# A transformer layer on one core: layer norms applied behind the projections, and one group's probabilities normalized by GpSimd

## The chip, the cores and the metric

The kernel runs on one core of one Trainium2 chip. The metric is the device time of one execution in microseconds. Where times are shown, they are the median of the runs beside their lowest and highest.

## The reference

x is 32 sequences of 512 rows of 256 float32 numbers. The layer is

```python
x = x + attn(layernorm(x), wq, wk, wv, wo, q_norm_w, k_norm_w)
x = x + ffn(layernorm(x), weight, gate_w, lora_U, lora_V)
```

with a layer norm without weights, (x - mean) / sqrt(var + 1e-5). attn has 16 query heads and 4 key and value heads of 64; q and k go through an RMS norm with a weight for each head (x * rsqrt(mean(x*x) + 1e-6) * w), a query sees itself and the 127 keys before it, and softmax runs over those. ffn is

```python
gate = softmax(xt @ gate_w.T)                       # 8 experts
base = xt @ weight.T                                # 256 x 256
t = einsum('nh,erh->ner', xt, lora_U)               # rank 16
out = base + (1/16) * einsum('ne,eor,ner->no', gate, lora_V, t)
```

## The kernel before

The 16384 rows are cut into 128 tiles of 128 rows; slot(T) = T % 4 is the place of tile T in its sequence. There is no loop that does one tile from end to end: each engine has a hand-written `step(T)`, a fixed list of operations on tiles T+4 to T-4, run for all T, and semaphores tie the engines together. Each engine does its list strictly in order, so an operation that waits holds everything behind it on that engine.

Products keep float32 precision by splitting both operands into a high and a low part of type fp32r and adding three matmuls (`three`, lines 627 to 629). The high part is written by ScalarE (`high_x`, `high_y`, `high_h`, `high_tg`, `high_weights`), the low one, the difference, by VectorE (`low_...`).

The path of a tile: the load into xs (SyncE's queue, line 170); mean and variance on VectorE (421 to 428); the power -0.5 on GpSimd (`x_rstd_power`, 215); xc = x - mean and xn = xc * rstd on GpSimd (220, 226); transposes of xn on TensorE (`transpose_x`, 637); projections to q (two halves of 512 columns) and k and v; ScalarE squares q and k, VectorE sums them (439, 461) and makes the mean squares (444, 467), GpSimd raises them to -0.5 (231, 237), VectorE scales (450, 473), TensorE transposes. v is copied out by ScalarE (298, 299).

Attention of a tile goes in four groups g of four heads: the scores (676), from slot 1 on a copy of the own half by ScalarE (`own_scores`, 323) and a merge by VectorE (481; in slot 0 one addition, 485), the maximum (491), the exponentials with their sums on ScalarE (330), the reciprocals (496), and the normalization of the probabilities: groups 0, 1 and 3 by one VectorE pass (`norm_probs`, 502), group 2 by four ScalarE activations (`normalise`, 339). TensorE transposes the probabilities (`transpose_probs`), ScalarE stores them as pT (345), GpSimd selects the part for the other keys (`select`, 253 and 255, not in slot 0), and TensorE multiplies with the values (695, 710).

Then come the projection with w_o, x1 = that + x (514), its statistics and h_rstd on GpSimd (519 to 526, 242), hn = (x1 - mean) * rstd by VectorE (`norm_h`, 531), its transposes (726), the ffn projection (ps_ffn: 256 columns of base, 128 of t, 8 of the gate), the gate's softmax (542, 361, 547, 552), tg (557), and `add_lora`, then ob = ps_ffn + x1 (569) and the store (195).

The order around the change. TensorE, in `step(T)`: the projections of T-2 with w_o, transposes of h(T-3), of k(T), ffn(T-3), transposes of x(T+1), attention and scores of group 0, transposes of the probabilities (T-1, 1), the first half of q(T+1), transposes of q(T), of tg(T-3), scores (T, 1), attention (T-1, 1), and then `transpose_probs(T - 1, 2)`; the second half of q(T+1) and the rest stand behind it. GpSimd, in the step of T-1 that runs beside it, has `select(T-1, 0)`, `x_rstd_power`, `low_value_difference`, `select(T-1, 1)`, `h_rstd_power(T - 2)`, `select(T-1, 2)`. VectorE reaches h_ve behind the merge of (T, 0), `gate_share`, `inverse(T-1, 3)`, `gate_t` and `low_y(T-1, 0)`, and does `norm_probs(T-1, 3)` right behind it. ScalarE has `gate_exp(T-3)` ahead of `own_scores(T, 0)`.

In the fill, `high_weights(0, 1, 2)` on ScalarE and `low_weights(0, 1, 2)` on VectorE stand ahead of all steps; VectorE's first statistics of x come behind them.

Of the kernel before, what the change touches and what calls it, by code (L numbers as in the profile page):

```python
# [26 lines left out]
CONSTANTS = 7  # L27
RING, DEEP, WIDE = 3, 4, 8
NORM_BY_ACT = (2,)
# [50 lines left out]
def layer(nc, x, w_qkv, w_o, w_ffn, w_v, norm_w, out):  # L80
    ctx = ExitStack()
    with ctx:
# [16 lines left out]
        ident, later_key, neg_later = sb("ident", [P, P]), sb("later_key", [P, P]), sb("neg_later", [P, P])  # L99
        minus_half = sb("minus_half", [P, HEADS])  # L100
# [3 lines left out]
        xc, xn = sb("xc", [P, DEEP, DIM]), sb("xn", [P, DEEP, DIM])  # L104
# [39 lines left out]
        s_s, s_own, s_merged, s_max, s_exp, s_rden, s_pn, s_pna = (sem(n) for n in ("scores_done", "own_scores_copied", "scores_merged", "max_done", "exp_done", "rden_done", "probs_normed", "probs_normed_by_act"))  # L144
        s_pt, s_pT, s_po, s_pv, s_yh, s_yl = (sem(n) for n in ("probs_transposed", "pT_stored", "pT_other_done", "pv_done", "yT_high", "yT_low"))
        s_o, s_x1, s_hst, s_hmv, s_hve, s_hrstd, s_hn, s_ht, s_hth, s_htl = (sem(n) for n in ("o_projected", "x1_done", "h_stats_done", "h_mean_done", "h_var_done", "h_rstd_done", "h_normed", "h_transposed", "hT_high", "hT_low"))
        s_ffn, s_gmax, s_gexp, s_grd, s_gate, s_tg, s_tt, s_tth, s_ttl, s_lv = (sem(n) for n in ("ffn_projected", "gate_max_done", "gate_exp_done", "gate_rden_done", "gate_done", "t_gated", "t_transposed", "tgT_high", "tgT_low", "lora_added"))
# [16 lines left out]

        @block.sync
        def _(sp):
            def load_x(T):
                if live(T):
                    wait(sp, s_x1, done(T - WIDE))
                    sp.dma_start(xs[:, T % WIDE], x[T * P:(T + 1) * P, :]).then_inc(s_x[T % WIDE], 16)  # L170

# [28 lines left out]
        def _(pool):  # L200
# [4 lines left out]
            pool.wait_ge(s_const, 4)  # L205
# [10 lines left out]

            def centre_x(T):
                if live(T):
                    pool.wait_ge(s_xmv, done(T))
                    pool.tensor_tensor(xc[:, T % DEEP], xs[:, T % WIDE], x_mv[:, T % DEEP, 0:1].to_broadcast([P, DIM]), ALU.subtract).then_inc(s_xc, 1)  # L220

            def norm_x(T):
                if live(T):
                    pool.wait_ge(s_xrstd, done(T))
                    pool.wait_ge(s_xc, done(T))
                    pool.tensor_tensor(xn[:, T % DEEP], xc[:, T % DEEP], x_rstd[:, T % DEEP].to_broadcast([P, DIM]), ALU.mult).then_inc(s_xn, 1)
# [49 lines left out]
        def _(act):  # L276
            def high_weights(*which):
                for n in which:
                    act.wait_ge(s_w[n], 128 if n == W_O else 16)
                    nc.scalar.activation(WEIGHTS[n][1], plain(n), ACT.Copy).then_inc(s_wh, 1)  # L280
# [588 lines left out]
```

## Time and profile before

| | us |
|---|---|
| median of 3 runs | 2423.46 (2421.21 to 2423.61) |
| the profiled execution | 2420.27 |
| its span, first to last instruction | 2418.6 |

| engine | busy us | share of the span |
|---|---|---|
| TensorE (PE) | 2380.1 | 98% |
| ScalarE (ACT) | 2160.9 | 89% |
| VectorE (DVE) | 2152.0 | 89% |
| GpSimd (POOL) | 1309.6 | 54% |

The profile is of one execution. PEld is TensorE's load of weights, beside PE. The end of a matmul is modelled, so a busy PE isn't PE at its peak; its starts are events. Lines such as L633 are lines of the kernel. "idle before <-" names what ended an engine's wait, by the semaphores.

### The profile page before, as it was taken

What the parts mean: (1) busy time and instruction counts of PE and PEld (TensorE: products, weight loads), DVE (VectorE), ACT (ScalarE), POOL (GpSimd) and SP (SyncE); (2) the same over time, 40 slices, a digit from 0 to 9 for tenths busy, and PEclk for the clock granted to TensorE, in tenths of its full rate; (3) what the DMA queues carried; (4) which work ended last, traced back from release to release, by engine and by line L of the source; (5) the groups of instructions that cost most, each with busy time, mean ns of one, the idle gap of its engine ahead of it and who ended that gap; (6) DMA issues with size and microseconds to landing.
All of it is one profiled execution on the core that took longest, in us unless ns stands there. A gap on an engine that the chain in (4) does not pass through costs nothing.

```text
span 2418.6 us, 70409 instructions
## 1 busy us (share of the span) xinstructions
PE 2380.1 (98%) x25856; PEld 1958.6 (81%) x25856; DVE 2152.0 (89%) x5736; ACT 2160.9 (89%) x7687; POOL 1309.6 (54%) x1771
## 2 busy tenths in 40 slices
PE   6999999999999999999999999999999999999997
PEld 4888888888888888888888888888888888888886
DVE  6899899999988999999999899989999998999886
ACT  5899989999998999899989989998999899899996
POOL 3555555555555555555555555555555555555542
PEclk9999999999999999999999999999999999999999
DMA  2000000000000000000000000000000000000000
GB/s 70 13 15 19 15 15 16 18 15 15 19 15 15 15 19 15 15 15 19 15 15 19 16 15 15 19 15 15 15 20 15 15 17 18 15 15 19 13 9 12
DMA packets 39729, 41.23 MB, mean 17 GB/s; under 512 B 4448, under 2 KB 38624, under 8 KB 39392
## 3 DMA queue, kind: packets, MB, share of 16 engines
q1 hardware_dynamic: 39392, 36.73, 5.0%
q8 instruction: 213, 3.49, 0.6%
q14 instruction: 124, 1.02, 0.1%
HBM read 19.93 MB, written 16.78 MB: 15 GB/s over the span
## 4 chain that ended last, share of the span: by engine, by line
PE 97%; issue 1%; ACT 1%; POOL 1%; DVE 1%; DMA 0%; SPq 0%; POOLq 0%
PE ps_a L633 17%; PE ps_scores L676 14%; PE ps_y L695 12%; PE ps_d L629 7%; PE ps_d L627 7%; PE ps_d L628 7%; PE ps_y L710 5%; PE ps_b L629 5%; PE ps_b L627 5%; PE ps_b L628 5%; PE ps_d L633 3%; PE ps_c L629 2%; PE ps_c L628 2%; PE ps_c L627 2%; PE ps_c L633 1%
## 5 line engine op out<-in xcount | busy, mean ns | idle before, releaser
L330 ACT ACTIVATE probs<-merged,neg_max 128x128 f32<-128x128 f32 x2048 | 796.0, 394 | 0.5 <-DVE neg_max L491 0.5
L253 POOL TENSOR_SCALAR_AFFINE_SELECT pT_other<-pT 128x256 f32<-128x256 f32 x384 | 173.1, 451 | 606.4 <-ACT pT L345 606.4
L237 POOL TENSOR_TENSOR q_r<-q_ve,minus_half 128x8 f32<-128x8 f32 x256 | 420.3, 1642 | 92.4 <-DVE q_ve L467 92.4
L676 PE MATMUL ps_scores<-kT,qT 64*64 64x192 f32 (+2 forms) x8192 | 415.2, 311 | 1.0 <-DVE merged L481 0.6
L330 ACT ACTIVATION_READ_ACCUMULATOR probs<-merged,neg_max 128x1 f32 x2048 | 396.5, 194 | 0.0
L481 DVE COPY_PREDICATED merged<-later_key,ps_scores 128x512 f32<-128x512 int32 x384 | 284.7, 741 | 106.2 <-ACT merged L323 106.2
L345 ACT ACTIVATE pT<-ps_a 128x512 f32<-128x512 f32 x512 | 306.2, 598 | 62.0 <-PE ps_a L633 61.1
L491 DVE TENSOR_REDUCE neg_max<-merged 128x4 f32<-128x512 f32 x512 | 346.5, 677 | 4.5
L695 PE MATMUL ps_y<-pT,values 128*64 128x128 f32 x4096 | 337.0, 285 | 1.8 <-ACT pT L345 1.8
L633 PE MATMUL ps_a<-ident,probs 128*128 128x128 f32 x2048 | 336.4, 287 | 0.0
L676 PEld LDWEIGHTS ps_scores<-kT,qT 64*64 64x64 f32 x8192 | 262.7, 133 | 60.6 <-issue 32.8
L627 PE MATMUL ps_d<-wo_h,yT_h 128*128 128x256 f32 x1024 | 309.0, 302 | 0.0
L633 PEld LDWEIGHTS ps_a<-ident,probs 128*128 128x128 f32 x2048 | 214.6, 140 | 101.8 <-issue 101.8
L695 PEld LDWEIGHTS ps_y<-pT,values 128*64 128x64 f32 x4096 | 213.2, 136 | 102.4 <-issue 100.1
L629 PE MATMUL ps_d<-wo_l,yT_h 128*128 128x256 f32 x1024 | 289.1, 282 | 0.0
L628 PE MATMUL ps_d<-wo_h,yT_l 128*128 128x256 f32 x1024 | 288.4, 282 | 0.0
L502 DVE TENSOR_TENSOR probs<-probs,rden 128x512 f32<-128x512 f32 x384 | 267.2, 696 | 8.7
L231 POOL TENSOR_TENSOR k_r<-k_ve,minus_half 128x4 f32<-128x4 f32 x128 | 129.6, 1012 | 217.0 <-DVE k_ve L444 217.0
L350 ACT ACTIVATE yT_h<-ps_y 128x256 fp32r<-128x256 f32 x512 | 197.1, 385 | 55.2 <-PE ps_y L710 39.5
L508 DVE TENSOR_TENSOR yT_l<-ps_y,yT_h 128x256 fp32r<-128x256 f32 x512 | 215.1, 420 | 31.6 <-ACT yT_h L350 26.3
L323 ACT ACTIVATE merged<-ps_scores 128x512 f32<-128x512 f32 x384 | 229.3, 597 | 8.9 <-PE ps_scores L676 2.4
L242 POOL TENSOR_TENSOR h_rstd<-h_ve,minus_half 128x1 f32<-128x1 f32 x128 | 119.8, 936 | 172.9 <-DVE h_ve L526 172.9
(114 smaller groups left out, 6175.7 us busy)
## 6 DMA issues: line engine op xcount, KB each, us to landing
xs<-x SPq DMA_DIRECT2D x128, 128.0 KB, 2.2
out<-ob SPq DMA_DIRECT2D x128, 128.0 KB, 1.7
w_plain<-w_qkv SPq DMA_DIRECT2D x3, 512.0 KB, 5.0
w_plain<-w_o SPq DMA_DIRECT2D x8, 128.0 KB, 5.3
w_plain<-w_ffn SPq DMA_DIRECT2D x1, 392.0 KB, 5.7
w_plain<-w_v SPq DMA_DIRECT2D x1, 128.0 KB, 4.9
nw<-norm_w SPq DMA_DIRECT2D x1, 1.0 KB, 5.5
```

Of the source, the lines that this page charges most:

```text
L237: pool.tensor_tensor(q_r[:, T % DEEP, c], q_ve[:, T % DEEP, c], minus_half[:, 0:8], ALU.pow).then_inc(s_qr[n], 1)
L330: last = nc.scalar.activation(probs[:, r, h], merged[:, r, h], ACT.Exp, bias=neg_max[:, r, h:h + 1], accum_out=den[:, r, h:h + 1])
L345: nc.scalar.activation(pT[:, ring(T, g)], ps_pT[:].rearrange("p (h q) -> p h q", h=REP), ACT.Copy).then_inc(s_pT, 1)
L481: nc.vector.copy_predicated(merged[:, ring(T, g)], later_key[:].bitcast(I32).unsqueeze(1).to_broadcast(every), ps_scores[:, :, 0:P]).then_ ...
L491: nc.vector.tensor_reduce(neg_max[:, ring(T, g)], merged[:, ring(T, g)], AX.X, ALU.max, negate=True).then_inc(s_max, 1)
L502: nc.vector.tensor_tensor(probs[:, r], probs[:, r], rden[:, r].unsqueeze(2).to_broadcast([P, REP, P]), ALU.mult).then_inc(s_pn, 1)
L627: nc.tensor.matmul(ps, stat_h, mov_h, start=first, stop=False, skip_group_check=onto_ended)
L628: nc.tensor.matmul(ps, stat_l, mov_h, start=False, stop=False, skip_group_check=onto_ended)
L629: return nc.tensor.matmul(ps, stat_h, mov_l, start=False, stop=last, skip_group_check=onto_ended)
L633: last = nc.tensor.transpose(ps[:, c * P:(c + 1) * P], src[:, c * P:(c + 1) * P], ident[:])
L676: last = nc.tensor.matmul(ps_scores[queries, 2 * half + c, first:end], qT[rows, T % 2, 2 * g + c, queries], kT[rows, g // 2, at + first:at ...
L695: last = nc.tensor.matmul(ps_y[HD * half:HD * half + HD, n, 0:P], values[:, T % WIDE, g // 2 * 2 + half], pT[:, ring(T, g), 2 * half:2 * h ...
```

## The change

- Four weights (the three parts of w_qkv and w_ffn) are centred once: TensorE multiplies a 128x128 matrix of 1/256 with each (two matmuls), which gives each column's mean on every partition, and VectorE subtracts it. Only then come the high and low parts. The banks used are cleared afterwards.
- x and x1 are transposed raw. `centre_x`, `norm_x` (GpSimd) and `norm_h` (VectorE) are gone.
- The factor rstd is applied later: in the copy of v (scale), in the exponential of the gate (scale), in the final sum (one scalar_tensor_tensor). For q and k it cancels in the RMS norm, whose epsilon becomes 1e-6 * (var + 1e-5), a new small VectorE operation, x_eps. The gate's maximum gets its factor in a new one, `gate_max_normed`.
- Group 2's probabilities are normalized by one GpSimd pass, `norm_by_pool`, between `h_rstd_power` and `select(T, 2)`, no more by ScalarE.
- The store of tile T-2 is issued behind the load of x(T+8), in place of the store of tile T.

```diff
@@ SyncE @@
-            for T in range(TILES):
+            for T in range(TILES + 2):
                 load_x(T + WIDE)
-                sp.wait_ge(s_ob, done(T))
-                sp.dma_start(out[T * P:(T + 1) * P, :], ob[:, T % 2]).then_inc(s_st[T % 2], 16)
+                store(T - 2)
@@ GpSimd @@
+            def norm_by_pool(T, g):
+                if live(T):
+                    r = ring(T, g)
+                    pool.wait_ge(s_rden, groups(T, g))
+                    pool.tensor_tensor(probs[:, r], probs[:, r], rden[:, r].unsqueeze(2).to_broadcast([P, REP, P]), ALU.mult).then_inc(s_pnp, 1)
...
             def step(T):
                 q_power(T + 1, 0)
                 select(T - 1, 3)
-                norm_x(T + 2)
                 k_power(T + 1)
                 q_power(T + 1, 1)
-                centre_x(T + 4)
                 select(T, 0)
                 x_rstd_power(T + 4)
                 low_value_difference(T + 1)
                 select(T, 1)
                 h_rstd_power(T - 1)
+                norm_by_pool(T, 2)
                 select(T, 2)
@@ ScalarE @@
+                    if n in CENTRED:
+                        act.wait_ge(s_wc, CENTRED.index(n) + 1)
...
+                    act.wait_ge(s_xrstd, done(T))
...
-                    nc.scalar.activation(g_exp[:, T % DEEP], ps_ffn[:, DIM + ER:FFN_OUT], ACT.Exp, bias=g_negmax[:, T % DEEP], accum_out=g_den[:, T % DEEP]).then_inc(s_gexp, 1)
+                    nc.scalar.activation(g_exp[:, T % DEEP], ps_ffn[:, DIM + ER:FFN_OUT], ACT.Exp, bias=g_negmax[:, T % DEEP], scale=h_rstd[:, T % DEEP], accum_out=g_den[:, T % DEEP]).then_inc(s_gexp, 1)
...
                 high_y(T - 1, 0)
-                normalise(T - 1, 2)
                 high_tg(T - 3)
@@ VectorE @@
-            nc.vector.memset(ps_scores[:], 0.0).then_inc(s_clear, 1)
+            def centre_weights(k):
+                dve.wait_ge(s_wm, k + 1)
+                w = plain(CENTRED[k])
+                nc.vector.tensor_tensor(w, w, mean_bank(k).unsqueeze(1).to_broadcast(w.shape), ALU.subtract).then_inc(s_wc, 1)
...
+                    nc.vector.tensor_scalar(x_eps[:, T % DEEP], x_mv[:, T % DEEP, 1:2], RMS_EPS, LN_EPS * RMS_EPS, ALU.mult, ALU.add).then_inc(s_xeps, 1)
...
+            def gate_max_normed(T):
+                if live(T):
+                    dve.wait_ge(s_gneg, done(T))
+                    dve.wait_ge(s_hrstd, done(T))
+                    nc.vector.tensor_tensor(g_negmax[:, T % DEEP], g_neg[:, T % DEEP], h_rstd[:, T % DEEP], ALU.mult).then_inc(s_gmax, 1)
...
                 maximum(T - 1, 1)
-                norm_h(T - 3)
                 add_x1(T - 4)
...
                 gate_max(T - 3)
+                gate_max_normed(T - 3)
                 low_x(T + 1)
...
-            low_weights(0, 1, 2)
+            for k in range(len(CENTRED)):
+                centre_weights(k)
+                if k < 3:
+                    low_weights(k)
+            dve.wait_ge(s_wc, len(CENTRED))
+            nc.vector.memset(ps_scores[:], 0.0).then_inc(s_clear, 1)
@@ TensorE @@
             def transpose_x(T):
-                pe.wait_ge(s_xn, done(T))
-                transpose_blocks(ps_xT, xn[:, T % DEEP], KC).then_inc(s_xt, 1)
+                pe.wait_ge(s_x[T % WIDE], 16 * (T // WIDE + 1))
+                transpose_blocks(ps_xT, xs[:, T % WIDE], KC).then_inc(s_xt, 1)
...
             def transpose_h(T):
-                pe.wait_ge(s_hn, done(T))
-                transpose_blocks(ps_hT, hn[:, T % 2], KC).then_inc(s_ht, 1)
+                pe.wait_ge(s_x1, done(T))
+                transpose_blocks(ps_hT, x1[:, T % DEEP], KC).then_inc(s_ht, 1)
...
+            def weight_means(k):
+                n = CENTRED[k]
+                pe.wait_ge(s_w[n], 16)
+                w = plain(n)
+                for c in range(KC):
+                    last = nc.tensor.matmul(mean_bank(k), mean_of[:], w[:, c], start=c == 0, stop=c == KC - 1)
+                last.then_inc(s_wm, 1)
```

## Rows read from the trace of the kernel before

**Rows 1.** Busy time by stretch: us and instructions (x) of each engine, clock, DMA.

```profile
25.00:50.00 25.00, 19.06 (x158) 13.17 (x160) 19.16 (x43) 16.92 (x58) 10.31 (x11) 0.80 0.01 1
...
200.00:1000.00 800.00, 800.00 (x8762) 660.25 (x8756) 723.53 (x1934) 726.97 (x2595) 443.82 (x599) 1.00 0.05 16
```

**Rows 2.** Timeline, one TensorE step, T-1 in slot 0: start, length, engine, operation.

```profile
1154.00 0.88 PE L676 MATMUL ps_scores<-kT,qT 64*64 64x192 f32 x16
...
1154.45 0.27 ACT L361 ACTIVATE g_exp<-ps_b,g_negmax 128x8 f32<-128x8 f32 x1 [0.55 <-DVE g_negmax L542]
...
1154.95 0.60 ACT L323 ACTIVATE merged<-ps_scores 128x512 f32<-128x512 f32 x1
...
1156.26 1.27 ACT L339 ACTIVATE probs<-probs,rden 128x128 f32<-128x128 f32 x4
...
1157.21 0.15 DVE L526 TENSOR_SCALAR h_ve<-h_mv 128x1 f32<-128x1 f32 x1
1157.28 0.68 DVE L502 TENSOR_TENSOR probs<-probs,rden 128x512 f32<-128x512 f32 x1
...
1157.44 0.94 POOL L242 TENSOR_TENSOR h_rstd<-h_ve,minus_half 128x1 f32<-128x1 f32 x1 [4.09 <-DVE h_ve L526]
...
1158.74 0.66 PE L633 MATMUL ps_a<-ident,probs 128*128 128x128 f32 x4
```

**Rows 3.** The same timeline in slot 2 (five rows), slot 3, slot 1.

```profile
1117.71 0.27 ACT L361 ACTIVATE g_exp<-ps_b,g_negmax 128x8 f32<-128x8 f32 x1 [0.79 <-DVE g_negmax L542]
...
1117.96 0.59 ACT L323 ACTIVATE merged<-ps_scores 128x512 f32<-128x512 f32 x1
...
1119.77 0.41 POOL L255 TENSOR_SCALAR_AFFINE_SELECT pT_other<-pT 128x256 f32<-128x256 f32 x1
...
1120.46 0.94 POOL L242 TENSOR_TENSOR h_rstd<-h_ve,minus_half 128x1 f32<-128x1 f32 x1 [0.27 <-DVE h_ve L526]
...
1122.18 0.66 PE L633 MATMUL ps_a<-ident,probs 128*128 128x128 f32 x4
...
1139.14 0.94 POOL L242 TENSOR_TENSOR h_rstd<-h_ve,minus_half 128x1 f32<-128x1 f32 x1 [0.24 <-DVE h_ve L526]
...
1140.68 0.66 PE L633 MATMUL ps_a<-ident,probs 128*128 128x128 f32 x4
...
1175.92 0.94 POOL L242 TENSOR_TENSOR h_rstd<-h_ve,minus_half 128x1 f32<-128x1 f32 x1 [0.67 <-DVE h_ve L526]
...
1177.23 0.66 PE L633 MATMUL ps_a<-ident,probs 128*128 128x128 f32 x4
```

**Rows 4.** Timeline of the fill.

```profile
2.07 0.29 POOL L209 TENSOR_SCALAR_AFFINE_SELECT neg_later<-neg_later 128x128 f32<-128x128 f32 x1
...
5.41 1.06 ACT L280 ACTIVATE wqkv_h<-w_plain 128x1024 fp32r<-128x1024 f32 x1 [3.33 <-DMA w_plain<-w_qkv]
...
6.58 3.78 DVE L416 TENSOR_TENSOR wqkv_l<-w_plain,wqkv_h 128x1024 fp32r<-128x1024 f32 x3 [4.57 <-ACT wqkv_h L280]
...
10.40 0.42 DVE L421 BATCH_NORM_STATS2 x_stats<-xs 128x6 f32<-128x256 f32 x1
...
11.69 0.55 POOL L215 TENSOR_TENSOR x_rstd<-x_ve,minus_half 128x1 f32<-128x1 f32 x1
...
13.30 0.61 POOL L226 TENSOR_TENSOR xn<-xc,x_rstd 128x256 f32<-128x256 f32 x1
...
14.06 0.66 PE L633 MATMUL ps_d<-ident,xn 128*128 128x128 f32 x2 [14.06 <-POOL xn L226]
...
15.57 0.43 DVE L421 BATCH_NORM_STATS2 x_stats<-xs 128x6 f32<-128x256 f32 x1 [2.88 <-DMA xs<-x]
...
16.32 0.42 DVE L433 TENSOR_TENSOR xT_l<-ps_d,xT_h 128x256 fp32r<-128x256 f32 x1
...
17.40 0.63 PE L628 MATMUL ps_d<-wqkv_h,xT_l 128*128 128x512 f32 x1
...
17.83 0.63 PE L629 MATMUL ps_d<-wqkv_l,xT_h 128*128 128x512 f32 x1
```

More of the change, by code:

```diff
@@ L26 @@
 MASKED = -1e30
[L27 removed]
+CONSTANTS = 8
 RING, DEEP, WIDE = 3, 4, 8
[L29 removed]
+NORM_BY_POOL = (2,)
 def live(t):
@@ L170, in load_x, with store @@
                     sp.dma_start(xs[:, T % WIDE], x[T * P:(T + 1) * P, :]).then_inc(s_x[T % WIDE], 16)
+            def store(T):
+                if live(T):
+                    sp.wait_ge(s_ob, done(T))
+                    sp.dma_start(out[T * P:(T + 1) * P, :], ob[:, T % 2]).then_inc(s_st[T % 2], 16)
             def load_weight(n):
@@ L332, in exps @@
                         last.then_inc(s_exp, 1)
-            def normalise(T, g):
-                if live(T):
-                    r = ring(T, g)
-                    act.wait_ge(s_rden, groups(T, g))
-                    for h in range(REP):
-                        last = nc.scalar.activation(probs[:, r, h], probs[:, r, h], ACT.Copy, scale=rden[:, r, h:h + 1])
-                    last.then_inc(s_pna, 1)
             def store_pT(T, g):
@@ L443, in k_mean_square @@
                     dve.wait_ge(s_kms, done(T))
-                    nc.vector.tensor_scalar(k_ve[:, T % DEEP], k_ms[:, T % DEEP], 1.0 / HD, RMS_EPS, ALU.mult, ALU.add).then_inc(s_kve, 1)
+                    dve.wait_ge(s_xeps, done(T))
+                    nc.vector.tensor_scalar(k_ve[:, T % DEEP], k_ms[:, T % DEEP], 1.0 / HD, x_eps[:, T % DEEP], ALU.mult, ALU.add).then_inc(s_kve, 1)
             def norm_k(T):
@@ L466, in q_mean_square @@
                     dve.wait_ge(s_qms[n], done(T))
-                    nc.vector.tensor_scalar(q_ve[:, T % DEEP, c], q_ms[:, T % DEEP, c], 1.0 / HD, RMS_EPS, ALU.mult, ALU.add).then_inc(s_qve[n], 1)
+                    dve.wait_ge(s_xeps, done(T))
+                    nc.vector.tensor_scalar(q_ve[:, T % DEEP, c], q_ms[:, T % DEEP, c], 1.0 / HD, x_eps[:, T % DEEP], ALU.mult, ALU.add).then_inc(s_qve[n], 1)
             def norm_q(T, n):
@@ L526, in h_mean_and_var @@
                     nc.vector.tensor_scalar_add(h_ve[:, T % DEEP], h_mv[:, T % DEEP, 1:2], LN_EPS).then_inc(s_hve, 1)
-            def norm_h(T):
-                if live(T):
-                    dve.wait_ge(s_hrstd, done(T))
-                    nc.vector.tensor_scalar(hn[:, T % 2], x1[:, T % DEEP], h_mv[:, T % DEEP, 0:1], h_rstd[:, T % DEEP], ALU.subtract, ALU.mult).then_inc(s_hn, 1)
             def low_h(T):
@@ L568, in add_x1 @@
                     wait(dve, s_st[T % 2], 16 * (T // 2))
-                    nc.vector.tensor_tensor(ob[:, T % 2], ps_ffn[:, 0:DIM], x1[:, T % DEEP], ALU.add).then_inc(s_ob, 1)
+                    nc.vector.scalar_tensor_tensor(ob[:, T % 2], ps_ffn[:, 0:DIM], h_rstd[:, T % DEEP], x1[:, T % DEEP], ALU.mult, ALU.add).then_inc(s_ob, 1)
             def step(T):
```

54 lines of the change are left out of this document (29 added, 25 removed).

## The prediction

> **What bounds the kernel now.** I read the windows first [rows 1]. Behind the fill, TensorE is busy 800.00 us of 800.00, at a full granted clock, while VectorE (723.53) and ScalarE (726.97) have 9% to spare and GpSimd (443.82) nearly half. So making VectorE or ScalarE lighter buys nothing there; only two things can move the time: a new wait that is long enough to reach TensorE's in-order queue, and the fill ahead of the loop, where TensorE is busy 19.06 of 25 us and the mean granted clock is 0.80.
>
> Next I read the timeline of one TensorE step, from the scores of group 0 of tile T to the transposes of group 2's probabilities of tile T-1 [rows 2] (here T-1 is the first tile of a sequence, slot 0), and of the three other slots [rows 3]. What to see: the scores end at 1154.88; ScalarE's copy starts at 1154.95, VectorE's merge and four short operations follow, and h_ve is done at 1157.36. GpSimd's h_rstd starts at 1157.44 and takes 0.94, to 1158.38. TensorE reaches the transposes of group 2 at 1158.74. This chain hangs on the scores of the same step, so it keeps its place relative to TensorE however long a step gets.
>
> **The change, part by part.**
>
> *Group 2's pass goes from ScalarE to GpSimd, behind h_rstd.* This is the term that decides. Before, ScalarE did it in 1.27 us from 1156.26 in that step, ended over a microsecond before the transposes, and waited only for the reciprocals. Now it stands in GpSimd's in-order queue behind h_rstd_power(T-1) of the same step, so it can't begin before 1158.38, 0.36 us ahead of the transposes that need it. TensorE will wait in every step; the price is
> stall = (start of h_rstd) + 0.94 + (the pass, d) - 0.04 + (release) - (start of the transposes).
> 0.04 is the overlap at which one GpSimd operation follows another. The release is 0.15: in the fill xn ended at 13.91 and its transposes started at 14.06 [rows 4].
>
> The trace has no 128x512 tensor_tensor on GpSimd. Nearest is xn, 128x256 with a broadcast operand, in 0.61 us [rows 4]. From below d is 0.61 (all of it fixed), from above 1.22 (all of it proportional). The selects grow from 0.29 (128 columns) [rows 4] to 0.41 (256 columns) [rows 3]: 0.12 to 0.13 for 128, so some 0.16 is fixed, and (0.61 - 0.16) x 2 + 0.16 = 1.06. I take d = 1.10, between that and the doubling, nearer the first. Could d be below the lower bound? Twice the elements don't take less.
> The Trainium skill (GPSIMD Engine Reference, section 3.1) gives 4497 ns for a tensor_tensor of 2048 fp32 columns on GpSimd and advises VectorE for such work; by that 512 columns are at least an estimated 1.12 us, and the sum would be 3 us longer.
>
> With d = 1.10 the sum in front of the transposes is 0.94 + 1.06 + 0.15 = 2.15 from h_rstd's start:
> slot 0: 1157.44 + 2.15 - 1158.74 = 0.85;
> slot 1: 1175.92 + 2.15 - 1177.23 = 0.84;
> slot 2: 1120.46 + 2.15 - 1122.18 = 0.43;
> slot 3: 1139.14 + 2.15 - 1140.68 = 0.61.
>
> *Small VectorE operations ahead of h_ve.* x_eps and gate_max_normed are 128x1 operations; h_ve is one of 0.15. An independent one adds some 0.07 (h_ve is followed by the next operation 0.07 behind its start, 1157.21 to 1157.28); a dependent one about 0.2 (0.15 and the wait for its own semaphore). Both stand ahead of gate_exp, which is queued on ScalarE ahead of the copy of the scores. In slot 0 the copy starts 0.50 behind gate_exp's start and needs only 0.25 (slot 2, where it follows at once: 1117.71 to 1117.96): cover 0.25, so 0.02 is left. In slot 2 all 0.27 shows. In slot 3 there is no such copy (0). In slot 1 I set the 0.27 against what the two GpSimd passes taken away release, and take -0.04. The stalls become 0.87, 0.80, 0.70 and 0.61, mean 0.75; in 127 steps 95 us.
>
> *What is removed.* centre_x and norm_x (0.61 each on GpSimd), norm_h (one VectorE pass a tile), ScalarE's four activations (1.27 a tile). All lie beside a TensorE that never waits [rows 1]: 0. Lighter queues don't shorten the chain, since its start is the scores' end. The transposes of x and x1 now wait for the load and for x1, both earlier than before: 0.
>
> *Scales moved into operations that are there* (store_v, gate_exp, the final add, the mean squares): same count and shape, 0; x_rstd and x_eps are four tiles ahead. *The SP queue*: out is stored two rounds later in program order, so a load of x stands only behind x1 of its tile. Stores come behind load_x(T+8), which waits for x1(T); ob(T-2) is ready in the same step, and its buffer is needed two steps later. Loads stay over one step ahead of their statistics. 0.
>
> *The fill.* Before: ScalarE rounds the first weight at 5.41, VectorE has three differences from 6.58 on (3.78 us), the first statistics start at 10.40, and the fourth round, held by the load of x, ends in low_x at 16.32; the first projection runs at once [rows 4]. After: each weight goes TensorE, VectorE, ScalarE, VectorE, in turn. Means: an fp32 matmul of 512 columns isn't in the trace. The fp32r one is issued every 0.43 us here, at the 1.2 GHz level (17.40 to 17.83). From below the fp32 one costs the same. From above: the fp32 scores are eight matmuls of 192 columns, four side by side on quarters of the array, in 0.88 [rows 2], so 384 columns in a row, 2.3 ns each at full clock, 4.6 at half: 2.35 for 512. That row holds one tail of some 0.27 besides, without which it is 1.6 and 1.65; I take 1.7. Two of them make 3.4, so centring can start at 8.9. Per weight then 1.25 (centre, like a difference, 1.23) + 1.15 (rounding 1.06) + 1.25 = 3.7, three times: 20.0; the centring of w_ffn 0.95; the clearing of the scores, moved here, 0.9; the norm weights 0.2: statistics start at 22.1. Four rounds of 0.85 (0.75 before, from the statistics at 15.57 to low_x at 16.32; x_eps and its wait on top): 25.5. low_x is 9.1 us later than 16.32. The matmul's bounds make this 6.6 to 10.4. The later parts of the fill hang on the same chain as before, shifted. TensorE has been idle since some 14 us by then, so the first projections run at 1.2 GHz as before.
>
> *The drain*: two gate chains with one more dependent operation, 0.2 each: 0.4.
>
> **The sum.** 2418.6 + 95 + 9.1 + 0.4 = 2523.1 us span; the profiled execution took 2420.27, 1.7 more than its span: 2524.8. The median of the runs shown is 2423.46, 3.2 above it and 0.13% away; I add 1.2 of that and say 2526.
>
> **The rivals.**
> A, the forecast: late pass, chance 0.70, with d from 0.87 to 1.22 between 2496 and 2540.
> B, the pass is short enough. Were d 0.61 and h_rstd 0.55, as x_rstd is at 11.69 [rows 4], the chain would be 0.55 + 0.57 + 0.15 = 1.27 from h_rstd's start; slots 0 and 1 leave 1.30, slot 3 more. Then only the fill is left: 2433. Against it: h_rstd takes 0.94 where VectorE's norm_probs overlaps it (1157.28 to 1157.96), and that is so in all four slots, unchanged by the diff. With d = 0.61 and h_rstd as it is the stall is 0.23 and the time some 2460. Chance 0.07.
> C, not slower: as B, and the fill is hidden as well, because the centring overlaps the loads (the fourth round waited for its x until 15.57) and the raw transposes of x no longer wait. It decides at a low_x at 20 us or sooner, with no stall left; then 2420 to 2427. Against it stand three serial round trips of 3.7. Chance 0.06, half of it faster.
> D, the pass is stretched by VectorE. The price is that of h_rstd, 0.94 - 0.55 = 0.39 a step: 50 us, 2576. For it: both engines will be at whole 128-row tiles. Against it: behind norm_probs VectorE has low_tg and two reduces in that stretch, and what stretched h_rstd was a pass with two SBUF operands. Chance 0.13.
> By the Trainium skill (SBUF — State Buffer, "SBUF: two separate sides") VectorE operations with two SBUF inputs and GpSimd exclude one another; h_rstd's 0.94 against 0.55 agrees. By that rule nothing in the stretch would hold up the pass.
> E, the waits bring down TensorE's clock. In [rows 1] it fell to a mean of 0.80 where TensorE idled for 6 us of 25; 0.75 us in 19 is far less. A mean of 0.97 would make it 3% more, 2600. Chance 0.04.
> The Trainium skill (TensorE: Matmul & The Clock Gate, "HAM oscillation") tells of kernels that fall back to the lower clock at each wait; the trace shows it only for the fill's waits.
>
> **How the numbers follow.** The range takes in A, its short-pass end and D: 2470 to 2590, leaving out B, C and the worst of E (0.16). A measurement of this kernel can tell 0.2% (5 us) from no change. A, B, D and E are all slower by more, 0.94; C gives 0.03 and 0.03.
>
> **What would show it.** The steady step longer by 0.6 to 0.9 us in each slot; in the waits, TensorE's ps_a transposes behind GpSimd's probs pass 120 to 128 times, in all 40 to 95 us (the modelled end of the matmul before covers a part of each); the pass on GpSimd 1.0 to 1.2 long, starting at h_rstd's end; the first projection near 26 us; ScalarE's share of busy time down by 7 points, to no avail. Wrong would be: h_rstd ends well ahead of the pass's need, the pass starts without waiting for it, or TensorE's wait comes from another engine.

## The result and the profile after

The changed kernel takes 2534.12 us (median of 4 runs, 2530.59 to 2534.84) against 2423.53 of the kernel before on the same chip (2421.21 to 2423.72): 1.0456 times as long, with an interval of 1.0438 to 1.0474. The forecast was 2526. The profiled span went from 2418.6 to 2533.0: 114.4 us.

The page of the kernel after: its span, busy time with the share of the span and the instructions (x), and the engines of the chain that ended last.

```profile
span 2533.0 us, 70415 instructions
...
PE 2408.9 (95%) x25872; PEld 1972.6 (78%) x25872; DVE 2156.3 (85%) x5868; ACT 2058.4 (81%) x7175; POOL 1259.0 (50%) x1644
...
PE 40%; DVE 24%; ACT 20%; POOL 10%; issue 6%; DMA 0%; SPq 0%; DVEq 0%; ACTq 0%
```

The chain of the kernel before was TensorE for 97% of the span. Now TensorE has 40% of it: it sets the pace no more. ScalarE's share of busy time is down from 89% to 81%, and that gave nothing back. Only half of these 8 points is work taken away (2160.9 us of busy time became 2058.4, 4 points of the old span); the rest comes from the longer span.

The windows of after, with the columns of [rows 1]; the last two are the drain.

```profile
200.00:1000.00 800.00, 772.24 (x8374) 635.75 (x8374) 693.71 (x1902) 664.86 (x2330) 407.18 (x525) 1.00 0.05 16
2490.00:2510.00 20.00, 14.93 (x163) 11.51 (x164) 11.05 (x29) 12.14 (x47) 5.85 (x12) 0.90 0.04 14
2510.00:2533.00 23.00, 13.51 (x74) 10.37 (x70) 6.36 (x22) 3.59 (x11) 1.33 (x3) 0.65 0.04 12
```

In the first row TensorE is busy for 772.24 us, where [rows 1] had 800.00, still at the full granted clock (1.00). The waits of after (what waited, for whom; us in all, times, longest) say whom it waits for:

```profile
PE ps_a L650 <- POOL probs L251: 85.1, 126, 1.1
PE ps_d L644 <- DVE xT_l L442: 10.4, 1, 10.4
```

126 waits for GpSimd's pass, in 128 tiles. How much longer a step became is read from the transposes of x, the same point of each step, 112 steps apart. Kernel before:

```profile
228.39 0.38 PE L633 MATMUL ps_d<-ident,xn 128*128 128x128 f32 x2
...
2299.83 0.38 PE L633 MATMUL ps_d<-ident,xn 128*128 128x128 f32 x2
```

Kernel after:

```profile
245.80 0.38 PE L650 MATMUL ps_d<-ident,xs 128*128 128x128 f32 x2
...
2405.33 0.38 PE L650 MATMUL ps_d<-ident,xs 128*128 128x128 f32 x2
```

2071.44 us became 2159.53: 88.1 in 112 steps, 0.787 a step. Ahead of them the change costs 17.4 (245.80 - 228.39), behind them the remaining 8.9. The same reading by slot gives, for T-1 in slots 0 to 3, steps of 18.057, 18.935, 18.927 and 18.061 before and of 18.946, 19.758, 19.812 and 18.607 after: +0.89, +0.82, +0.88, +0.55. "Steps" below are always these four, in this order.

The timeline of a step with T-1 in slot 0, as in [rows 2] (start, length, engine, operation, idle time before it and what ended it):

```profile
1210.59 0.88 PE L693 MATMUL ps_scores<-kT,qT 64*64 64x192 f32 x16
...
1211.30 0.36 ACT L366 ACTIVATE g_exp<-ps_b,g_negmax,h_rstd 128x8 f32<-128x8 f32 x1 [0.80 <-DVE g_negmax L554]
...
1211.65 0.58 ACT L336 ACTIVATE merged<-ps_scores 128x512 f32<-128x512 f32 x1
...
1213.96 0.68 DVE L513 TENSOR_TENSOR probs<-probs,rden 128x512 f32<-128x512 f32 x1
...
1214.12 0.94 POOL L245 TENSOR_TENSOR h_rstd<-h_ve,minus_half 128x1 f32<-128x1 f32 x1 [4.71 <-DVE h_ve L537]
...
1215.04 1.03 POOL L251 TENSOR_TENSOR probs<-probs,rden 128x512 f32<-128x512 f32 x1
...
1216.22 0.63 PE L650 MATMUL ps_a<-ident,probs 128*128 128x128 f32 x4 [0.82 <-POOL probs L251]
```

GpSimd idles for 4.71 us before h_rstd, and then the pass that TensorE wants has to queue behind it. h_rstd starts 3.53 behind the scores (3.44 in [rows 2]), the transposes 5.63 (4.74). The pass lasts 1.03, and its data are in TensorE's hands 0.15 after its end.

The same in slots 2, 3 and 1, to be set beside [rows 3]:

```profile
1173.16 0.36 ACT L366 ACTIVATE g_exp<-ps_b,g_negmax,h_rstd 128x8 f32<-128x8 f32 x1 [0.85 <-DVE g_negmax L554]
...
1173.51 0.59 ACT L336 ACTIVATE merged<-ps_scores 128x512 f32<-128x512 f32 x1
...
1174.77 0.33 DVE L564 TENSOR_SCALAR gate<-g_exp,g_rden 128x8 f32<-128x8 f32 x1
...
1176.12 0.93 POOL L245 TENSOR_TENSOR h_rstd<-h_ve,minus_half 128x1 f32<-128x1 f32 x1 [0.67 <-DVE h_ve L537]
1177.02 1.03 POOL L251 TENSOR_TENSOR probs<-probs,rden 128x512 f32<-128x512 f32 x1
...
1178.20 0.63 PE L650 MATMUL ps_a<-ident,probs 128*128 128x128 f32 x4 [0.71 <-POOL probs L251]
...
1197.27 0.63 PE L650 MATMUL ps_a<-ident,probs 128*128 128x128 f32 x4 [0.46 <-POOL probs L251]
...
1235.54 0.63 PE L650 MATMUL ps_a<-ident,probs 128*128 128x128 f32 x4 [0.70 <-POOL probs L251]
```

The idle time shown (0.46 to 0.82) is less than what the step grows by (0.55 to 0.89), because the modelled end of the matmul before covers 0.07 to 0.17 of it. So the sum of the waits, 85.1, understates the loss.

The fill of after, beside [rows 4]:

```profile
5.22 3.75 PE L768 MATMUL ps_y<-w_plain,mean_of 128*128 128x512 f32 x4 [5.22 <-DMA w_plain<-w_qkv]
...
9.09 1.22 DVE L419 TENSOR_TENSOR w_plain<-w_plain,ps_y 128x1024 f32<-128x1024 f32 x1 [9.09 <-PE ps_y L768]
...
10.35 1.06 ACT L291 ACTIVATE wqkv_h<-w_plain 128x1024 fp32r<-128x1024 f32 x1 [8.27 <-DVE w_plain L419]
...
18.40 1.23 DVE L424 TENSOR_TENSOR wqkv_l<-w_plain,wqkv_h 128x1024 fp32r<-128x1024 f32 x1 [1.12 <-ACT wqkv_h L291]
...
21.63 0.42 DVE L429 BATCH_NORM_STATS2 x_stats<-xs 128x6 f32<-128x256 f32 x1
...
24.82 0.41 DVE L442 TENSOR_TENSOR xT_l<-ps_d,xT_h 128x256 fp32r<-128x256 f32 x1
...
25.34 0.77 PE L644 MATMUL ps_d<-wqkv_h,xT_h 128*128 128x512 f32 x1 [10.43 <-DVE xT_l L442]
```

Three round trips between TensorE, VectorE and ScalarE delay low_x from 16.32 to 24.82 (+8.5); the first projection follows at 25.34.

### The profile page after: what moved, and what is told of

It is laid out like the page before. It is cut to its first block, busy times and chain, and to the rows that moved or that the text cites. A ratio compares the mean times of both kernels' runs of the same rounds, so it can differ in the third digit from the quotient of the medians.

```text
span 2533.0 us, 70415 instructions
## 1 busy us (share of the span) xinstructions
PE 2408.9 (95%) x25872; PEld 1972.6 (78%) x25872; DVE 2156.3 (85%) x5868; ACT 2058.4 (81%) x7175; POOL 1259.0 (50%) x1644
## 4 chain that ended last, share of the span: by engine, by line
PE 40%; DVE 24%; ACT 20%; POOL 10%; issue 6%; DMA 0%; SPq 0%; DVEq 0%; ACTq 0%
PE ps_a L650 8%; PE ps_y L714 5%; POOL probs L251 5%; ACT probs L343 5%; DVE merged L492 5%; POOL h_rstd L245 5%; PE ps_scores L693 4%; ACT merged L336 4%; PE ps_y L729 3%; ACT pT L350 3%; PE ps_b L644 3%; DVE probs L513 3%; PE ps_b L645 3%; PE ps_b L646 3%; PE ps_d L650 2%
## 5 line engine op out<-in xcount | busy, mean ns | idle before, releaser
L262 POOL TENSOR_SCALAR_AFFINE_SELECT pT_other<-pT 128x256 f32<-128x256 f32 x384 | 160.2, 417 | 640.7 <-ACT pT L350 640.7
L650 PE MATMUL ps_a<-ident,probs 128*128 128x128 f32 x2048 | 333.6, 286 | 85.2 <-POOL probs L251 85.1
L714 PEld LDWEIGHTS ps_y<-pT,values 128*64 128x64 f32 x4096 | 214.1, 136 | 103.1 <-issue 100.7
```

The lines of the kernel that those rows point to most:

```text
L650: last = nc.tensor.transpose(ps[:, c * P:(c + 1) * P], src[:, c * P:(c + 1) * P], ident[:])
L714: last = nc.tensor.matmul(ps_y[HD * half:HD * half + HD, n, 0:P], values[:, T % WIDE, g // 2 * 2 + half], pT[:, ring(T, g), 2 * half:2 * h ...
```

## The experiments

The theory: nearly all the loss is GpSimd's pass standing behind h_rstd, and the place costs, not the pass (some 100 us); the centring costs 8 to 9 in the fill (the stretch before all engines are at work); the rest costs next to nothing. The rivals: the layer-norm part (new products, scale operands, raw transposes) carries a part of the 0.79 a step; the pass costs by its work on GpSimd wherever it stands; VectorE stretches it.

### The layer norms alone, and the pass alone

First kernel: after, with group 2 normalized by ScalarE at its old place.

```
# GpSimd's step
-                norm_by_pool(T, 2)
# ScalarE's step (normalise as in the kernel before)
                 high_y(T - 1, 0)
+                normalise(T - 1, 2)
```

> The changed kernel with group 2 normalized by ScalarE again, at its old place; the layer norms stay behind the projections. Theory (TensorE waits in each step for the GpSimd pass, 0.79 us, and the rest is fill): the waits behind GpSimd's probs go, what is left is the later fill, some 9 us: 2432 to 2438, steady steps at 18.06 and 18.93 us as before. Rival 1 (the moved layer norms, with their added VectorE operations, carry the loss): over 2500.

Measured: 2443.25 us, ratio 1.0083 (1.0066 to 1.0101); steps 18.067, 19.047, 19.064, 18.107. The 90 us are gone, but it lies 5 us above the upper end of what I expected. A part of that is a wait that I had not foreseen, in slots 1 and 2, at the transposes of tg. This kernel in slot 2 (as in the fences that follow, the first number is the start, the second the length):

```profile
1206.14 0.36 ACT L373 ACTIVATE g_exp<-ps_b,g_negmax,h_rstd 128x8 f32<-128x8 f32 x1 [0.85 <-DVE g_negmax L562]
...
1207.64 0.42 POOL L262 TENSOR_SCALAR_AFFINE_SELECT pT_other<-pT 128x256 f32<-128x256 f32 x1 [3.38 <-ACT pT L357]
1207.75 0.34 DVE L572 TENSOR_SCALAR gate<-g_exp,g_rden 128x8 f32<-128x8 f32 x1
...
1208.56 0.30 PE L658 MATMUL ps_c<-ident,tg 128*128 128x128 f32 x1
```

The kernel before in slot 2, same operations (its g_exp took 0.27, from 1191.69):

```profile
1193.21 0.22 DVE L552 TENSOR_SCALAR gate<-g_exp,g_rden 128x8 f32<-128x8 f32 x1
1193.38 0.41 POOL L253 TENSOR_SCALAR_AFFINE_SELECT pT_other<-pT 128x256 f32<-128x256 f32 x1 [2.54 <-ACT pT L345]
...
1194.34 0.27 PE L633 MATMUL ps_c<-ident,tg 128*128 128x128 f32 x1
```

From the transposes of x, where the step begins, those of tg come at 4.24 before and at 4.30 here. gate_max_normed and a longer g_exp delay ScalarE's copy of the scores, with it VectorE's merge and gate; gate then falls beside GpSimd's select and takes 0.34 instead of 0.22. Before, in this slot, it was just ahead of it. The steps in slots 1 and 2 grow by 0.11 and 0.14, of which 0.07 and 0.09 stand at the transposes of tg (in slot 2 the matmul behind them starts 4.536 behind the transposes of x, 4.447 before; medians); the rest stands elsewhere in the step (see the tenth kernel).

Second kernel: before, with group 2 on GpSimd behind h_rstd and nothing else changed.

```
# GpSimd's step
                 h_rstd_power(T - 1)
+                norm_by_pool(T, 2)
                 select(T, 2)
# ScalarE's step
-                normalise(T - 1, 2)
```

> The kernel before with one edit: group 2 normalized by one GpSimd pass right behind h_rstd_power, ScalarE's four activations taken away. Theory: with the measured pass of 1.035 the sum ahead of the transposes is 0.94 + 1.0 + 0.15 = 2.09 from h_rstd's start, so the stalls are 0.79, 0.78, 0.37 and 0.55 in slots 0 to 3, mean 0.62, 79 us: 2500 to 2508, less than the changed kernel since the two small VectorE operations aren't there. Rival 1: under 2445.

Measured: 2500.72, ratio 1.0321 (1.0305 to 1.0336), within the expected 2500 to 2508; steps 18.837, 19.701, 19.273, 18.581, that is +0.78, +0.77, +0.35, +0.52. This is the formula with d = 1.03 and no delay ahead of h_ve: in slots 0 to 3 it gives 0.78, 0.77, 0.36, 0.54. By the ratios the pass in this place costs 78 us alone, the rest of the change 20 alone, and both together 110: some 12 us come from their meeting, since a delay of h_ve costs nothing until the pass hangs on it. Most of it is in slot 2: +0.35 here, +0.14 in the first kernel, +0.88 in after.

### The pass in another place, and half of it

Third kernel: the pass of after, two places earlier in GpSimd's order, ahead of `select(T, 1)` and `h_rstd_power`.

```
                 low_value_difference(T + 1)
+                norm_by_pool(T, 2)
                 select(T, 1)
                 h_rstd_power(T - 1)
-                norm_by_pool(T, 2)
                 select(T, 2)
```

> The changed kernel with the GpSimd pass two places earlier in its queue, ahead of select(T, 1) and h_rstd_power. Theory (it is the place in the queue, not the pass): the pass starts at its reciprocals, about 2.2 us into the step, and ends near 3.3, over 2 us before the transposes: no wait, 2432 to 2438, as with ScalarE. Rival 2 (a pass of 128x512 on GpSimd costs TensorE time wherever it stands, by its length or through VectorE): over 2480.

Measured: 2442.25, ratio 1.0078 (1.0063 to 1.0093); steps 18.067, 19.046, 19.064, 18.121, within 0.014 of the first kernel's. Its timeline in slot 0:

```profile
1169.42 1.04 POOL L251 TENSOR_TENSOR probs<-probs,rden 128x512 f32<-128x512 f32 x1 [2.35 <-DVE rden L507]
...
1171.79 0.94 POOL L245 TENSOR_TENSOR h_rstd<-h_ve,minus_half 128x1 f32<-128x1 f32 x1 [1.33 <-DVE h_ve L537]
...
1172.99 0.65 PE L650 MATMUL ps_a<-ident,probs 128*128 128x128 f32 x4
```

The pass takes 1.04 as in after, starts as soon as the reciprocals are there and is done 2.5 us before TensorE asks; GpSimd still idles for 1.33 before h_rstd. The work on GpSimd is free, the place cost 92 us. That rules out the rival by which the work itself costs. The time is 4 us above the expected 2432 to 2438; this excess over the expectation is that of the first kernel, so it belongs to the layer-norm part.

Fourth kernel: the pass in its place, but only for heads 0 and 1; ScalarE does the other two.

```
-  pool.tensor_tensor(probs[:, r], probs[:, r], rden[:, r].unsqueeze(2)...([P, REP, P]), ALU.mult)
+  pool.tensor_tensor(probs[:, r, 0:2], probs[:, r, 0:2], rden[:, r, 0:2].unsqueeze(2)...([P, 2, P]), ALU.mult)
...
+  for h in range(2, REP):       # ScalarE, normalise(T - 1, 2)
```

> The changed kernel with the GpSimd pass cut to heads 0 and 1 (128x256, about 0.6 us) at its place behind h_rstd; ScalarE does heads 2 and 3 at the old place. Theory: each step's wait falls by what the pass gets shorter, 0.43 us, to 0.45, 0.41, 0.45 and 0.12: 54 us less, 2476 to 2486. Rival 2 with a fixed cost for any GpSimd pass in that place: little changed, over 2510. Rival 3 (something else ends the wait): no change.

Measured: 2478.15, ratio 1.0227 (1.0212 to 1.0242), within the expected 2476 to 2486; steps 18.507, 19.344, 19.384, 18.193: +0.45, +0.41, +0.46, +0.13. Its timeline in slot 0:

```profile
1188.89 0.94 POOL L245 TENSOR_TENSOR h_rstd<-h_ve,minus_half 128x1 f32<-128x1 f32 x1 [4.71 <-DVE h_ve L546]
1189.80 0.61 POOL L251 TENSOR_TENSOR probs<-probs,rden 128x256 f32<-128x256 f32 x1
...
1190.55 0.63 PE L659 MATMUL ps_a<-ident,probs 128*128 128x128 f32 x4 [0.40 <-POOL probs L251]
```

The pass is 0.42 shorter (0.61 for 1.03), the steps 0.41 to 0.44: what TensorE waits for is the end of the pass.

### What stretches h_rstd

Fifth kernel: after, with VectorE's norm_probs of group 3 two operations later, out of h_rstd's way.

```
                 h_mean_and_var(T - 2)
-                norm_probs(T - 1, 3)
                 low_tg(T - 3)
                 maximum(T, 0)
+                norm_probs(T - 1, 3)
                 sum_q(T + 1, 0)
```

> The changed kernel with VectorE's norm_probs(T-1, 3) moved two places back in its own list, behind low_tg and maximum(T, 0), so that it no longer starts beside h_rstd. Theory (h_rstd's 0.93 us holds 0.39 of waiting for VectorE's pass with two SBUF operands; uncontended it takes 0.55): h_rstd takes 0.55, the GpSimd pass starts 0.39 earlier and holds its 1.03, VectorE's pass now waits for it, harmlessly. TensorE's wait falls by 0.39 a step: 50 us less than the changed kernel, 2480 to 2490. If h_rstd is 0.93 for another reason: no change, 2534.

Measured: 2490.45, ratio 1.0282 (1.0265 to 1.0299; before 2422.07); steps 18.562, 19.475, 19.435, 18.240. Its timeline in slot 0:

```profile
1192.15 0.56 POOL L245 TENSOR_TENSOR h_rstd<-h_ve,minus_half 128x1 f32<-128x1 f32 x1 [4.72 <-DVE h_ve L537]
1192.67 1.04 POOL L251 TENSOR_TENSOR probs<-probs,rden 128x512 f32<-128x512 f32 x1
1193.15 1.11 DVE L513 TENSOR_TENSOR probs<-probs,rden 128x512 f32<-128x512 f32 x1
...
1193.86 0.63 PE L650 MATMUL ps_a<-ident,probs 128*128 128x128 f32 x4 [0.46 <-POOL probs L251]
```

h_rstd takes 0.56, not 0.94, the step is 0.38 shorter in slot 0 (0.28 to 0.38 in the others), and the time falls by 42 us by the ratios. I had expected 50 less, 2480 to 2490. Now it is VectorE's product that shows 1.11 instead of 0.68, since it is issued while GpSimd's pass runs: it ends 0.55 behind that pass. These VectorE operations with two SBUF inputs and GpSimd's don't run side by side here: whichever comes second pays. By the Trainium skill (SBUF — State Buffer, "SBUF: two separate sides") such VectorE operations and GpSimd exclude one another; this run agrees in both directions, 0.94 against 0.56 and 1.11 against 0.68.

### The small operations ahead of h_ve

Sixth kernel: after without the product that makes the gate's maximum ready; the exponential takes the raw one (softmax is the same with either shift).

```
-                gate_max_normed(T - 3)
...
-  nc.scalar.activation(g_exp[...], ..., ACT.Exp, bias=g_negmax[...], scale=h_rstd[...], ...)
+  nc.scalar.activation(g_exp[...], ..., ACT.Exp, bias=g_neg[...], scale=h_rstd[...], ...)
```

> The changed kernel without gate_max_normed: the gate's exponential takes the raw maximum as bias (a softmax doesn't depend on its bias) and waits for h_rstd itself. Theory: ScalarE's copy of the scores starts 0.1 to 0.2 us earlier in slots 0 to 2, and the chain to h_rstd with it, so TensorE's wait falls by 0.1 in slot 0 and 0.2 in slots 1 and 2: mean 0.12, 16 us less, 2515 to 2522. Were the pass's place the only cause, and its chain bound by the scores alone: no change, 2534.

Measured: 2525.44, ratio 1.0428 (1.0412 to 1.0443); steps 18.840, 19.726, 19.712, 18.625. By the ratios that is 7 us less than after (8.7 in microseconds, but `before` was 1.5 faster beside this run), where I expected 12 to 19: a miss. Rows of this kernel show what stayed. The columns of the first: form, count; busy us, mean ns; idle before.

```profile
L367 ACT ACTIVATE g_exp<-ps_b,g_neg,h_rstd 128x8 f32<-128x8 f32 x128 | 45.9, 359 | 70.7 <-DVE g_neg L549 69.0
```

The other two, in slot 2:

```profile
1170.11 0.42 POOL L262 TENSOR_SCALAR_AFFINE_SELECT pT_other<-pT 128x256 f32<-128x256 f32 x1 [3.29 <-ACT pT L350]
1170.13 0.42 DVE L565 TENSOR_SCALAR gate<-g_exp,g_rden 128x8 f32<-128x8 f32 x1
```

The exponential still takes 0.36 (0.27 before): what lengthened it is the scale operand, not the product. And gate now starts with the select and takes 0.42: it starts earlier and ends where the select ends, so that half of the gain is lost again.

### The centring

Seventh kernel: the first one (ScalarE normalizes group 2) without the centring of the weights; that part of the computation is left out. The clearing of the scores also goes back to its place in the kernel before, ahead of everything on VectorE.

```
-            for k in range(len(CENTRED)):
-                centre_weights(k)
-                if k < 3:
-                    low_weights(k)
+            low_weights(0, 1, 2)
# and, on TensorE:
-            for k in range(len(CENTRED)):
-                weight_means(k)
```

> As e1_ln_only, and the weights are not centred (that part of the computation is left out: the four means and subtractions of the fill); all else is as in e1. Theory: the centring's serial round trips make the first projection 8.5 us later, so this gives 2433 to 2436, and what is left above the kernel before is the steady wait of e1 (9.6 us) and the drain (1). If the fill doesn't carry through: 2443.

Measured: 2436.95, ratio 1.0058 (1.0043 to 1.0073); first projection at 17.57 us (25.16 with centring), span 2431.6 (2438.8). So the centring, with the clearing that had moved behind it, costs 7.2 us by the spans and 6 by the ratios (1.0083 and 1.0058): the fill's term. The median is just above the expected 2433 to 2436.

### Mending it

Eighth kernel: the third and sixth edits together, the earlier pass and no product.

> As e3_pass_earlier, and without gate_max_normed as in e6. Theory: of e3's 18 us over the kernel before, 9.6 come from transpose_tg, which waits 0.1 us for tg in slots 1 and 2 because the gate's product delays the copy of the scores ahead of it; they go: 2431 to 2435, steady steps at 18.06 and 18.93. Rival (they come from x_eps or from the raw transposes): 2442 as e3.

Measured: 2435.86, ratio 1.0055 (1.0040 to 1.0070), just above the expected 2431 to 2435; steps 18.067, 18.967, 18.968, 18.106. The wait for tg is gone from slots 1 and 2 (0.08 and 0.10 a step less than with the product, 19.046 and 19.064; over 127 steps 5.6 us, where I had expected 9.6). What remains is 0.01 to 0.045 a step, and the fill.

Ninth kernel: the same with the fill in another order: the two halves of q first, low_x and the first steps' work between the centrings, w_ffn's centring and the clearing of the scores after the first projections.

```
+            centre_weights(0)
+            step(-4)
+            low_weights(0)
+            centre_weights(1)
+            step(-3)
+            centre_weights(2)
+            low_x(0)
+            low_weights(1, 2)
+            step(-2)
...
```

> As e9 (GpSimd pass earlier, no product for the gate), and the fill in another order: the weights in the order of their use, VectorE centres and splits the first weight, then does the first x rounds and low_x(0) between the other weights, and the centring of w_ffn and the clearing of the scores stand in the first step beside GpSimd's power. Theory: the first projection starts near 16.5 us in place of 25.1 and the fill costs what it cost before; 7 to 9 us less than e9: 2426 to 2430, within 0.3% of the kernel before. If the fill is bound by TensorE's clock instead: under 4 us gained.

Measured: 2425.28, ratio 1.0009 (1.0000 to 1.0017), just below the expected 2426 to 2430. Its first projections:

```profile
16.15 0.47 PE L657 MATMUL ps_d<-wqkv_h,xT_h 128*128 128x512 f32 x1 [2.12 <-DVE xT_l L446]
...
16.46 0.40 PE L658 MATMUL ps_d<-wqkv_h,xT_l 128*128 128x512 f32 x1
...
16.69 0.40 PE L659 MATMUL ps_d<-wqkv_l,xT_h 128*128 128x512 f32 x1
```

They start at 16.15, 9 us earlier than in after, and follow one another every 0.23 us, against 0.43 at the 1.2 GHz level [rows 4]: TensorE is at 2.4 GHz here (granted clock 1.00 from 15 to 20 us). By the ratios the new order gives 11 us, more than the 7.2 of the centring: the earlier start and the higher clock come together, and no run parts them. The centring can be hidden after all, but not in the order it was given.

Tenth kernel: the eighth with the buffers at the addresses of before (new buffers behind the old ones, the unused ones kept):

```
-        mean_of = sb("mean_of", [P, P])
...
+        xc, xn = sb("xc", [P, DEEP, DIM]), sb("xn", [P, DEEP, DIM])
...
         ob = sb("ob", [P, 2, DIM])
+        mean_of, x_eps, g_neg = sb("mean_of", [P, P]), sb("x_eps", [P, DEEP, 1]), sb("g_neg", [P, DEEP, 1])
```

> As e9, with the buffers xc, xn and hn allocated again, unused, and the new ones at the end, so that the buffers TensorE reads (up to ob) lie where they lay before. The matmuls of e9 and e7 are issued 0.04 us a step later in all, spread over the fp32r ones. If that comes from the addresses: steady steps 18.06, 18.93, 18.93, 18.06 and 4 to 5 us less than e9, 2431. If not: as e9, 2435 to 2436.

Measured: 2434.32, ratio 1.0046 (1.0032 to 1.0060), for an expected 2431; steps 18.052, 18.976, 18.975, 18.063. Mostly a miss. Slots 0 and 3 are back at the lengths of before (18.057, 18.061), slots 1 and 2 are still 0.04 and 0.05 longer. Over 112 steps that is 1.2 us of the 3.6 that were to be explained. The trace shows where the rest lies, and it isn't the wait for tg any more (the matmul behind its transposes starts 4.447 behind those of x in slot 2, just as before). It lies at two pairs of transposes: in slot 2 the two of x1 stand 0.131 us apart for 0.108 before, the two of k 0.147 for 0.110 (medians of 25 steps; 0.108 each in slots 0 and 3 of both kernels). What holds them up, and by what the addresses cost 0.043 in slot 3, stays open.

Eleventh kernel: the ninth with those addresses, and x_eps at the end of VectorE's step.

```
-  nc.vector.tensor_scalar(x_eps[...], x_mv[...], RMS_EPS, LN_EPS * RMS_EPS, ...)   # in x_mean_and_var(T + 4)
...
                 sum_q(T + 1, 0)
+                x_epsilon(T + 4)
```

> e8 with the addresses of e10 and x_eps moved to the end of VectorE's step. Theory: TensorE's steady steps are those of the kernel before to 0.02 us, so no more than the fill and drain can differ: 2420 to 2427, the same as the kernel before within 0.2%. It can't be faster by more than that, since TensorE's own work is unchanged.

Measured: 2422.96, ratio 1.0002 (0.9994 to 1.0011): the same as before, as expected. The steps are those of the tenth kernel (18.052, 18.969, 18.978, 18.060), so the place of x_eps changes nothing, and the expected 0.02 us to the steps of before is missed in slots 1 and 2: 2.2 us in the 112 steps (2073.63 for 2071.44), which these runs can't tell from none. Its windows show why it can't be faster:

```profile
200.00:1000.00 800.00, 800.00 (x8736) 659.82 (x8734) 720.56 (x1931) 695.44 (x2420) 426.87 (x555) 1.00 0.05 16
```

ScalarE 695.44 where [rows 1] has 726.97, GpSimd 426.87 for 443.82, and TensorE 800.00 as before. The change as an idea makes three engines lighter and leaves the one that bounds the kernel as it was; its best is no change.

## Why the prediction was right, and where it was off

*The late pass: right in mechanism and place, its size by errors that partly cancel.* Forecast stalls were 0.87, 0.80, 0.70 and 0.61 (mean 0.75), measured 0.89, 0.82, 0.88 and 0.55 (0.787), in all 101 us (88.1 in the 112 steps, 7.9 ahead of them, 4.7 behind) for the 95 of the sum. The third kernel shows the place as the cause, the fourth the pass's length, the second that the late pass alone costs 78 us.

*Its terms.* h_rstd took 0.93 to 0.94, as forecast from before. The pass, d, was taken as 1.10 and is 1.035: 0.065 too long, 8 us too much. Its estimate from a small fixed part of the selects (1.06) was better than the choice above it. By the figure of the Trainium skill (GPSIMD Engine Reference, section 3.1) it was to be at least an estimated 1.12; with this form, whose second operand is a broadcast reciprocal, the trace has 1.035. The release is 0.145 to 0.15.

*The delay ahead of h_ve: too small by nearly half in slot 2.* The step took 0.27 for the two 128x1 operations. From the scores' start to h_rstd's start slot 2 had 3.45 before (1117.01 is that scores' start, 1120.46 h_rstd) and 3.95 in after (1172.17, 1176.12): 0.50. Of it the copy of the scores starts 0.39 later, and 0.11 is gate's 0.33 for 0.22. The failed step is the sentence "Scales moved into operations that are there ... same count and shape, 0": a scale operand makes the exponential 0.36 long instead of 0.27, ahead of the copy, and the delay moves gate beside the select. The same sentence covers the copy of v, whose 256 pieces went from a mean of 0.374 us to 0.466, without effect on the time. With 0.50 and d = 1.035 the formula gives 0.43 + 0.50 - 0.065 = 0.87 for slot 2; measured 0.88. In slot 0 the cover of 0.25 held, but the exponential's 0.09 came on top (0.09 later for a forecast 0.02). In slot 1 the forecast was -0.04, from a relief by the GpSimd passes taken away that was only guessed: h_rstd's start, 3.86 behind the scores' before (1172.06, 1175.92), is 3.91 in after (1229.54, 1233.45), 0.05 later; with that the formula gives 0.84 + 0.05 - 0.065 = 0.825 (measured 0.82). In slot 3 the delay was 0 (0.61 - 0.065 = 0.545; measured 0.55).

*What the 0 for the small operations hid.* Where the pass is not late, the same delay makes the transposes of tg wait in slots 1 and 2: the first and the third kernel pay some 6 us (5.6 by the eighth kernel's steps) that the prediction had nowhere, and their expectations repeated the error. In after, that wait lies in the shadow of the greater one.

*The removed work: right that it buys nothing.* ScalarE's four activations, norm_h, centre_x and norm_x brought nothing, in every kernel. The 7 points less on ScalarE were too many: the activations taken away are 135 us of busy time (2192.1 in the first kernel, 2057.2 in the third), but the scale operands put 31 back (2160.9 before, 2192.1 in the first kernel), which leaves 4 points at an equal span.

*The fill: right.* The sums of a weight's columns take four matmul records 0.86 apart where I counted two of 1.7, the same 3.4. Centring could start at 9.09 (forecast 8.9), statistics at 21.63 (22.1), low_x began at 24.82 (25.5; 0.5 of the difference comes from the statistics). At tile 12's transposes, ten waits of 0.787 behind, 17.4 - 7.9 = 9.5 are left (forecast 9.1). The seventh kernel puts 7.2 of that on the centring and the clearing moved behind it. That it can't be hidden was a property of this order only; rival C's bound, a low_x at 20 us or sooner, is met in the ninth kernel, whose first projection runs at 16.15; with no late pass it lands at 2425, within C's 2420 to 2427.

*The drain: 0.4 forecast, some 4.2 measured.* Behind the transposes of tile 124 there are 8.9 us more, of which six waits make 4.7. The dependent products and the longer exponential give an estimated 0.5. For the rest the windows show a lower clock: 0.90 and 0.65 in the last two stretches of after, 1.00 and 0.75 in the stretches of the kernel before that answer to them (2380 to 2400, 2400 to 2419). TensorE is at 1.2 GHz there for one stretch more than before. The second, fifth and sixth kernels, with whole late passes, have 0.86 to 0.94 between 43 and 23 us before their end; the first, third and fourth, with none or half of one, have 1.00. But the eighth kernel, without a late pass, has 0.91 there (2392 to 2412) and 0.71 behind it. So the waits go with the fall of the clock but aren't shown to be its cause; that stays open.

*The sum.* 100.7 + 9.5 + 4.2 make the 114.4 measured, for 104.5 forecast. The difference of 9.9 is 8 too much for d, 13 too little for the delays (7 of it in slot 2), and 4 too little for the drain, with small ones. So two errors of the steady state partly cancel: that the total is closer than its terms is luck.

*The rivals.* Two small sums of B don't follow from the terms: 2526 less 95 is 2431, not 2433, and d = 0.61 with h_rstd as it is leaves a mean stall of 0.25, not 0.23. B and D are excluded by one row: a pass of 1.03 in after. It is not 0.61, and it has the same length at another place in the queue (1.04 in the third kernel), so nothing stretches it; beside it VectorE has two reduces, as the prediction said. VectorE's product could even be pushed beside it, and then VectorE waited (fifth kernel). E is excluded too: TensorE's clock stays at 1.00 with a wait of 0.8 in every 19 us. The Trainium skill (TensorE: Matmul & The Clock Gate, "HAM oscillation") tells of a kernel that falls back in every round, at waits for a DMA that are several times as long as those here; the steady state of after shows no fall at waits under 1 us. The prediction's remark that the trace shows such a fall only in the fill overlooked the drain of the kernel before, at 0.75.

## What to carry to other kernels

Work that moves to an idle engine is priced by its place in that engine's queue: look at what stands ahead of it there, when that can start, and when the consumer needs the result; the same pass cost 92 us behind h_rstd and nothing two places earlier. An operation ahead of a chain that has no slack must be priced with its operands too, not by count and shape alone: a scale operand made one 0.09 us longer here. And where one engine is busy all the time, lightening the others has a best case of no change, so any new dependence can only be paid for.

## What the runs showed that was not expected

- A per-partition operand costs time in small operations: ScalarE's 128x8 exponential 0.267 us with a bias alone, 0.358 with a scale from SBUF as well (mean of 128 each). The copy of v, 256 columns, went from 0.374 to 0.466 with a scale: 0.09 again, at another width. The 128x4 mean squares on VectorE 0.158 with a constant and 0.220 with x_eps; the final 128x256 sum 0.414, and 0.484 as a product and a sum.
- A 128x8 tensor_scalar on VectorE with such an operand takes 0.22 us alone and 0.33 to 0.44 when it starts beside a GpSimd select, whose own 0.41 to 0.42 don't change. In the rows above it ends 0.02 to 0.03 behind the select, whenever it began (1208.09 for 1208.06, 1170.55 for 1170.53): its end hangs on the select's, not on its own start.
- GpSimd's product with a broadcast operand: 0.61 us for 256 columns, 1.035 for 512; if it grows evenly, an estimated 0.19 is fixed.
- The addresses of the buffers alone move a step by up to 0.043 us (18.106 in the eighth kernel, 18.063 in the tenth, slot 3).
- fp32 matmuls of 512 columns: the four records of a weight take 3.75 us at the 1.2 GHz level and 1.88 at 2.4 GHz.
